# A scale-free attention block and a five-matrix feed-forward on eight cores: the transposed-weight reloads move to SyncE's queue, and one weight copy moves from VectorE to ScalarE

## The chip, the cores and the metric

The kernel runs on the 8 cores of one Trainium2 chip. Every core runs the same program on its own data, without any exchange between cores. The time is the device time of the slowest core in microseconds (us). A core has TensorE (PE: matmuls and, here, also all transposes, which are matmuls against an identity), VectorE (DVE), ScalarE (ACT), GpSimd (POOL) and SyncE (SP, which only issues DMAs here). Each engine runs its own instruction list strictly in the order in which the program wrote it; a DMA is issued by an instruction on POOL, SP or ACT, and lands later, which a semaphore tells.

## What is computed

There are 16384 tokens of 1024 numbers. All cores need the 64x64 matrix `energy` over all tokens; after that, each core owns 2048 tokens.

```
Q, K, V = x wq', x wk', x wv'                    # 64 wide
energy  = K' V                                    # 64 x 64, over all 16384 tokens
x1 = layernorm(x + sqrt(3/64) * Q energy wo')
h  = silu(s1 * (x1 w1')) * (s2 * (x1 w2'))        # 4096 wide
h  = gelu(sh1 * (h h1'))                          # 4096 x 4096 weights
h  = gelu(sh2 * (h h2'))                          # 4096 x 4096 weights
y  = layernorm(x1 + s3 * (h w3'))                 # back to 1024
```

## The kernel before

The tokens of a core are worked in two halves, `h = 0` and `h = 1`, of 1024 tokens each. A half goes through these stages in order:

- `emit_b3(h)`: for 8 tiles of 128 tokens, the attention output, the residual sum and the first layer norm. SyncE loads a tile of x into `X1R` (line 392) and stores the normed tile to `x1s` in device memory (line 422). TensorE transposes the tile into `X1T`.
- `emit_stage1(h)`: 32 output chunks `oc` of 128 hidden units. For each, 16 matmuls for w1 and w2 on tokens 0 to 511 (lines 525 and 533, into `PA`), then 16 on tokens 512 to 1023 (into `PB`). ScalarE applies silu (line 540), VectorE multiplies (line 545) into `HB`.
- `emit_big_stage` three times, for h1 (32 chunks), h2 (32) and w3 (8): 64 matmuls per chunk (line 621), alternating between `PA` and `PB`, and one activation on ScalarE (line 645).
- `make_final_ln`: the last layer norm over 8 tiles.

**First half.** The weights arrive untransposed as f32 and are cast to bf16 by POOL's DMAs into `WSB` (lines 462, 466, 563). TensorE transposes each chunk into the PSUM tiles `PT[0]` and `PT[1]`, and these are copied into one of two slots of `WTB`. In `emit_stage1` the w1 part is copied by VectorE (line 491) and the w2 part by ScalarE (line 495). ScalarE then issues a DMA that stores the transposed chunk to device memory (`wt12`, line 502; `h1t`, `h2t` and `w3t` in the big stages).

**Second half.** Nothing is transposed again. The stored chunk is loaded back into a slot of `WTB`: 512 KB for each of the 32 chunks of `emit_stage1` (line 509) and 1024 KB for each of the 72 chunks of the big stages (line 571). These loads are issued by POOL, whose list holds nothing else then. The load of chunk `oc` waits until the matmuls of chunk `oc - 2` have left the slot, so that it lands while chunk `oc - 1` is computed. TensorE waits for it just before the first matmul of `oc`.

**The last layer norm of the first half** is woven into `emit_stage1(1)` by a hook: before each of the chunks 0, 4, 8, ... 28, `fstep0(oc // 4)` writes one tile of it into the lists. TensorE transposes the tile out of `GB` (line 666), ScalarE copies it to `FT` (line 675), VectorE adds the residual `X1R` (line 693), then `emit_ln` runs: ScalarE (338, 342), VectorE (347, 352), ScalarE's square root (357), VectorE (362, 366, 371). SyncE's list gets, for each tile, first the load of `X1R` (line 683), then a wait for the end of the tile's norm (line 371) and the store of `y` (line 705). The hook is called ahead of everything else that a chunk writes:

```
        for oc in range(HC):
            if hook is not None:
                hook(oc)
            ...
                w('y', 'v', lnv)
            ...
                em('y', lambda s_, th=th, r=r: s_.dma_start(
                    out=y[th * 128:(th + 1) * 128, :],
```

`w(q, src, val)` (line 144) makes engine `q` wait for a semaphore; `'g'` is POOL, `'y'` SyncE, `'t'` TensorE, `'s'` ScalarE and `'v'` VectorE. `light_handoff` puts such waits between stages. In the second half the gate that it gets is the end of all TensorE work of the stage before, so the first load of each big stage starts when the stage before has ended.

Of the kernel before, what the change touches and what calls it, by code (L numbers as in the profile page):

```python
# [16 lines left out]
EC = E // 128  # L17
# [11 lines left out]
def build():  # L29
# [58 lines left out]
    SGP = [EE(nc.semaphore("SGP0")), EE(nc.semaphore("SGP1")),  # L88
           EE(nc.semaphore("SGP2")), EE(nc.semaphore("SGP3"))]
    SYL = [EE(nc.semaphore("SYL0")), EE(nc.semaphore("SYL1"))]  # L90
    SYS = [EE(nc.semaphore("SYS0")), EE(nc.semaphore("SYS1"))]
    SWS = [EE(nc.semaphore("SWS0")), EE(nc.semaphore("SWS1"))]
    SUS = [EE(nc.semaphore("SUS0")), EE(nc.semaphore("SUS1"))]
# [4 lines left out]

    Q = {k: [] for k in "gystv"}
    C = {"l": 0, "g0": 0, "g1": 0, "g2": 0, "g3": 0,  # L100
# [3 lines left out]
    SEM = {"l": SL, "g0": SGP[0], "g1": SGP[1], "g2": SGP[2], "g3": SGP[3],  # L104
           "y0": SYL[0], "y1": SYL[1],
           "z0": SYS[0], "z1": SYS[1],
           "w0": SWS[0], "w1": SWS[1], "u0": SUS[0], "u1": SUS[1],
# [34 lines left out]
    def w(q, src, val):  # L142
        if val > 0:
            em(q, lambda e, s=SEM[src], v=val: e.wait_ge(s, v))

# [4 lines left out]
    def fi(ins, fin, sem=None):  # L150
        if fin:
            ins.then_inc(sem if sem is not None else ST, 1)
        return ins

    QENG = {"l": "g", "g0": "g", "g1": "g", "g2": "g", "g3": "g",
            "y0": "y", "y1": "y",
            "z0": "y", "z1": "y",
            "w0": "s", "w1": "s", "u0": "s", "u1": "s",
# [291 lines left out]
                x1te[tp] = inc('s')  # L450
        return C['s']

    def emit_stage1(h, hook=None):
        wdma = {}; wtp = {}; wte = {}; wte_lo = {}; mmv = {}; sil = {}; hv = {}; cw = {}
        for oc in range(HC):
            if hook is not None:
                hook(oc)
            ro = oc % 2
            if h == 0:
                if oc >= 2:  # L460
                    w('g', 't', wtp[oc - 2])
                em('g', lambda g, oc=oc, ro=ro: g.dma_start(
                    out=WSB[:, ro * 1024:(ro + 1) * 1024],
                    in_=w1[oc * 128:(oc + 1) * 128, :]).then_inc(SGP[ro], 16))
                inc(f'g{ro}', 16)
                em('g', lambda g, oc=oc, ro=ro: g.dma_start(
                    out=WSB[:, 2048 + ro * 1024: 2048 + (ro + 1) * 1024],
                    in_=w2[oc * 128:(oc + 1) * 128, :]).then_inc(SGP[ro], 16))
                wdma[oc] = inc(f'g{ro}', 16)
                w('t', f'g{ro}', wdma[oc])  # L470
                if oc >= 1:
                    w('t', 's', wte[oc - 1])
                    w('t', 'v', wte_lo[oc - 1])
                for c in range(EC):
                    em('t', lambda t, ro=ro, c=c: t.transpose(
                        PT[0][:, c * 128:(c + 1) * 128],
                        WSB[:, ro * 1024 + c * 128: ro * 1024 + (c + 1) * 128], IDB[:]))
                for c in range(EC):
                    em('t', lambda t, ro=ro, c=c: fi(t.transpose(
                        PT[1][:, c * 128:(c + 1) * 128],  # L480
                        WSB[:, 2048 + ro * 1024 + c * 128: 2048 + ro * 1024 + (c + 1) * 128],
                        IDB[:]), c == EC - 1))
                wtp[oc] = inc('t')
                w('v', 't', wtp[oc])
                w('s', 't', wtp[oc])
                if oc >= 2:
                    w('v', 't', mmv[(oc - 2, 1)])
                    w('v', f'w{ro}', cw[oc - 2])
                    w('s', 't', mmv[(oc - 2, 1)])
                    w('s', f'w{ro}', cw[oc - 2])  # L490
                em('v', lambda v, ro=ro: v.tensor_copy(  # L491
                    WTB[:, ro * 2048: ro * 2048 + 1024],
                    PT[0][:, 0:1024]).then_inc(SV, 1))
                wte1 = inc('v')
                em('s', lambda s, ro=ro: s.copy(
                    WTB[:, ro * 2048 + 1024: ro * 2048 + 2048],
                    PT[1][:, 0:1024]).then_inc(SS, 1))
                wte[oc] = inc('s')
                wte_lo[oc] = wte1
                w('s', 'v', wte1)  # L500
                w('s', 's', wte[oc])
                em('s', lambda s, oc=oc, ro=ro: s.dma_start(
                    out=wt12[oc],
                    in_=WTB[:, ro * 2048:(ro + 1) * 2048]).then_inc(SWS[ro], 16))
                cw[oc] = inc(f'w{ro}', 16)
            else:
                if oc >= 2:
                    w('g', 't', mmv[(oc - 2, 1)])
                em('g', lambda g, oc=oc, ro=ro: g.dma_start(
                    out=WTB[:, ro * 2048:(ro + 1) * 2048],  # L510
                    in_=wt12[oc]).then_inc(SGP[ro], 16))
                wdma[oc] = inc(f'g{ro}', 16)
            for g_i in range(2):
                s_ = oc * 2 + g_i
                rp = s_ % 2
                if g_i == 0:
                    if h == 0:
                        w('t', 'v', wte_lo[oc])
                    else:
                        w('t', f'g{ro}', wdma[oc])  # L520
                if s_ >= 2:
                    w('t', 's', sil[s_ - 2])
                    w('t', 'v', hv[s_ - 2])
                for c in range(EC):
                    em('t', lambda t, ro=ro, rp=rp, c=c, g_i=g_i: t.matmul(  # L525
                        PP[rp][:, 0:512],
                        WTB[:, ro * 2048 + c * 128: ro * 2048 + (c + 1) * 128],
                        X1T[:, c * 1024 + g_i * 512: c * 1024 + g_i * 512 + 512],
                        start=(c == 0), stop=(c == EC - 1)))
                if g_i == 0 and h == 0:  # L530
                    w('t', 's', wte[oc])
                for c in range(EC):
                    em('t', lambda t, ro=ro, rp=rp, c=c, g_i=g_i: fi(t.matmul(  # L533
                        PP[rp][:, 512:1024],
                        WTB[:, ro * 2048 + 1024 + c * 128: ro * 2048 + 1024 + (c + 1) * 128],
                        X1T[:, c * 1024 + g_i * 512: c * 1024 + g_i * 512 + 512],
                        start=(c == 0), stop=(c == EC - 1)), c == EC - 1))
                mmv[(oc, g_i)] = inc('t')
                w('s', 't', mmv[(oc, g_i)])
                em('s', lambda s, rp=rp, g_i=g_i, oc=oc: s.activation(  # L540
                    TS1[:, g_i * 512:(g_i + 1) * 512], PP[rp][:, 0:512], AF.Silu,
                    bias=0.0, scale=SC1[:, oc:oc + 1]).then_inc(SS, 1))
                sil[s_] = inc('s')
                w('v', 's', sil[s_])
                em('v', lambda v, rp=rp, g_i=g_i, oc=oc: v.scalar_tensor_tensor(
                    HB[:, oc * 1024 + g_i * 512: oc * 1024 + g_i * 512 + 512],
                    PP[rp][:, 512:1024], SC2[:, oc:oc + 1],
                    TS1[:, g_i * 512:(g_i + 1) * 512],
                    ALU.mult, ALU.mult).then_inc(SV, 1))
                hv[s_] = inc('v')  # L550
        return wtp.get(HC - 1, C['t'])

    def emit_big_stage(wsrc, scl, src_buf, dst_buf, nout, func, cache, h):
        wdma = {}; wtp = {}; wte = {}; mmv = {}; gel = {}; cw = {}; rdv = {}
        for oc in range(nout):
            so = oc % 2
# [10 lines left out]
                    wdma[(oc, half)] = inc(f'g{s_slot}', 16)  # L567
            else:
                if oc >= 2:
                    w('g', 't', mmv[(oc - 2, 3)])  # L570
                em('g', lambda g, oc=oc, so=so, cache=cache: g.dma_start(
                    out=WTB[:, so * H:(so + 1) * H],
                    in_=cache[oc]).then_inc(SGP[so], 16))
                rdv[oc] = inc(f'g{so}', 16)

            def emit_tp(b):
                half = b // 2
# [29 lines left out]
            def emit_mm(b):  # L607
                rp = oc % 2
                if h == 0:
                    w('t', 'v', wte[(oc, b)])  # L610
                elif b == 0:
                    w('t', f'g{so}', rdv[oc])
                if b == 0 and oc >= 2:
                    w('t', 's', gel[oc - 2])
                for j in range(8):
# [117 lines left out]
    for h in range(2):  # L733
# [3 lines left out]
        if h == 0:  # L737
            g1_ = emit_stage1(0)
        else:
            fstep0 = make_final_ln(0)  # L740
            g1_ = emit_stage1(1, hook=lambda oc: fstep0(oc // 4) if oc % 4 == 0 else None)
        light_handoff(g1_)
        g2_ = emit_big_stage(h1, SCH1, HB, GB, HC, AF.Gelu, h1t, h)
        light_handoff(g2_)
        g3_ = emit_big_stage(h2, SCH2, GB, HB, HC, AF.Gelu, h2t, h)
        light_handoff(g3_)
        g4_ = emit_big_stage(w3, SC3, HB, GB, EC, AF.Copy, w3t, h)
        if h == 0:
            light_handoff(g4_)
        else:  # L750
# [42 lines left out]
```

## Time and profile before

| | us |
|---|---|
| median of three runs | 3510.24 |
| the three runs | 3510.24, 3539.15, 3329.22 |
| the profiled execution | 3328.28 |
| its span on the slowest core (core 6) | 3326.7 |
| spans of the eight cores | 3311.9 to 3326.7 |

The profile is one execution, recorded on the slowest core. Its page has the busy time of each engine, the span in 40 slices, the chain of waits that ended last, and groups of instructions by line. The trace behind it also answers for a stretch of time: which instruction ran when, and what ended the idle time ahead of it. Times in it are counted from the start of the span. By these, the stages lie at about 287 to 372 us (`emit_b3(0)`), 372 to 682 (`emit_stage1(0)`), 682 to 1880 (big stages, first half), 1880 to 1965 (`emit_b3(1)`), 1965 to 2214 (`emit_stage1(1)` with the hook), 2214 to 3234 (big stages, second half), and 3234 to the end (last layer norm of the second half). What comes before 287 us is the pass over all 16384 tokens.

### The profile page before, as it was taken

The page shows a single profiled execution, that of the slowest core. Times are in us where ns is not written, and L with a number is a line of the kernel's source. Part 1 is how long each engine was busy: PE and PEld are TensorE (multiplying, and loading weights), DVE is VectorE, ACT ScalarE, POOL GpSimd, SP SyncE. Part 2 cuts the span into 40 slices and gives each one's busy share as a digit, 9 for nine tenths or more (in the row PEclk, how much of TensorE's full clock was granted, in tenths as well). Part 3 has the DMA queues.
Part 4 walks back from the last instruction along what each step waited for, and adds up shares of the span by engine and source line. Part 5 has one row for each costly group of instructions (what it writes and reads, how often), then busy time and mean ns, then how long its engine had stood idle before and what let it go on. Part 6 is the DMA issues. An engine that isn't in the chain of part 4 may idle for free.

```text
span 3326.7 us, 40570 instructions; the slowest of 8 cores (3311.9 to 3326.7 us)
## 1 busy us (share of the span) xinstructions
PE 2855.8 (86%) x16601; PEld 1447.9 (44%) x16601; DVE 448.5 (13%) x833; ACT 527.0 (16%) x630; POOL 243.3 (7%) x460
## 2 busy tenths in 40 slices
PE   5673588889999999999999649989999999999990
PEld 4662244444444444444444324434444444444440
DVE  1112222211111111111111232210000000000002
ACT  4553222210000000000000123320000000000012
POOL 3220011100000000000000000000000000000000
PEclk9886799999999999999999869999999999999995
DMA  8994455556666656655555423222222122222112
GB/s 110 136 135 102 97 110 106 114 109 127 128 131 136 127 123 131 131 127 127 127 126 127 119 96 104 96 92 76 76 76 76 64 78 78 78 78 78 68 57 95
DMA packets 89170, 347.16 MB, mean 104 GB/s; under 512 B 10904, under 2 KB 10976, under 8 KB 70560
## 3 DMA queue, kind: packets, MB, share of 16 engines
q0 software_dynamic: 64800, 218.73, 34.8%
q10 hardware_dynamic: 14976, 92.28, 6.8%
q1 hardware_dynamic: 9216, 33.56, 2.9%
q8 instruction: 138, 2.26, 0.3%
q14 instruction: 40, 0.33, 0.0%
HBM read 361.83 MB, written 109.05 MB: 142 GB/s over the span
## 4 chain that ended last, share of the span: by engine, by line
PE 75%; DVE 5%; DMA 4%; issue 3%; ACT 3%; DVEq 0%; SPq 0%; ACTq 0%; POOL 0%; POOLq 0%
PE PA L621 30%; PE PB L621 29%; PE PT L585 3%; PE PA L525 3%; PE PA L533 3%; PE PB L533 3%; PE PB L525 3%; DMA X1R<-x 2%; DVE WTB L596 1%; DMA X1R<-x1s 1%; ACT TS L540 1%; DVE WTB L491 1%; ACT TS L342 1%; DVE X1F L411 1%; DVE X1F L371 1%
## 5 line engine op out<-in xcount | busy, mean ns | idle before, releaser
L621 PE MATMUL PA<-HB,WTB 128*128 128x512 bf16 x2560 | 571.6, 383 | 12.1 <-DMA WTB<-h1t 6.3
L621 PE MATMUL PB<-HB,WTB 128*128 128x512 bf16 x2560 | 562.3, 379 | 0.0
L621 PE MATMUL PA<-GB,WTB 128*128 128x512 bf16 x2048 | 452.3, 380 | 5.8 <-DMA WTB<-h2t 5.8
L621 PE MATMUL PB<-GB,WTB 128*128 128x512 bf16 x2048 | 449.9, 379 | 0.0
L621 PEld LDWEIGHTS PA<-HB,WTB 128*128 128x128 bf16 x2560 | 250.9, 99 | 312.3 <-issue 25.3
L621 PEld LDWEIGHTS PB<-HB,WTB 128*128 128x128 bf16 x2560 | 248.9, 98 | 292.5
L596 DVE COPY WTB<-PT 128x1024 bf16<-128x1024 bf16 x288 | 192.5, 689 | 990.8 <-PE PT L585 990.7
L621 PEld LDWEIGHTS PA<-GB,WTB 128*128 128x128 bf16 x2048 | 199.7, 98 | 241.9 <-issue 9.6
L621 PEld LDWEIGHTS PB<-GB,WTB 128*128 128x128 bf16 x2048 | 198.9, 98 | 234.2
L585 PE MATMUL PT<-IDB,WSB 128*128 128x128 bf16 x2304 | 164.9, 220 | 53.7 <-DVE WTB L596 44.4
L525 PE MATMUL PA<-X1T,WTB 128*128 128x512 bf16 x512 | 125.8, 390 | 72.0 <-DVE WTB L491 52.7
L585 PEld LDWEIGHTS PT<-IDB,WSB 128*128 128x128 bf16 x2304 | 142.6, 98 | 98.9 <-issue 65.6
L257 PE MATMUL PT<-IDB,XB 128*128 128x128 bf16 x1024 | 91.3, 241 | 78.5 <-DMA XB<-x 68.7
L693 DVE SCALAR_TENSOR_TENSOR X1F<-X1R,FT 128x1024 f32<-128x1024 f32 x12 | 14.7, 1225 | 1045.4 <-DMA X1R<-x1s 1038.1
L265 ACT COPY XT<-PT 128x1024 bf16<-128x1024 bf16 x128 | 129.5, 1012 | 126.2 <-PE PT L257 125.2
L563 POOL DMA_DIRECT2D WSB<-h x128 | 68.9, 538 | 990.4 <-PE PT L585 938.7
L440 PE MATMUL PT<-IDB,X1B 128*128 128x128 bf16 x128 | 16.2, 305 | 135.3 <-DVE X1B L429 135.3
L533 PE MATMUL PA<-X1T,WTB 128*128 128x512 bf16 x512 | 123.4, 385 | 0.0
L525 PE MATMUL PB<-X1T,WTB 128*128 128x512 bf16 x512 | 121.0, 379 | 0.0
L533 PE MATMUL PB<-X1T,WTB 128*128 128x512 bf16 x512 | 120.9, 379 | 0.0
L645 ACT ACTIVATE HB<-PA,SCH 128x1024 bf16<-128x1024 f32 x32 | 35.7, 1114 | 458.5 <-PE PA L621 458.5
L257 PEld LDWEIGHTS PT<-IDB,XB 128*128 128x128 bf16 x1024 | 69.1, 107 | 88.1 <-issue 84.5
(116 smaller groups left out, 1341.9 us busy)
## 6 DMA issues: line engine op xcount, KB each, us to landing
WSB<-h POOLq DMA_DIRECT2D x128, 512.0 KB, 6.3
XB<-x POOLq DMA_DIRECT2D x128, 256.0 KB, 6.1
h1t<-WTB ACTq DMA_DIRECT2D x32, 1024.0 KB, 8.3
h2t<-WTB ACTq DMA_DIRECT2D x32, 1024.0 KB, 8.4
WTB<-h1t POOLq DMA_DIRECT2D x32, 1024.0 KB, 5.1
WTB<-h2t POOLq DMA_DIRECT2D x32, 1024.0 KB, 5.1
WSB<-w POOLq DMA_DIRECT2D x64, 256.0 KB, 6.0
wt<-WTB ACTq DMA_DIRECT2D x32, 512.0 KB, 6.6
```

Of the source, the lines that this page charges most:

```text
L257: em('t', lambda t, r2=r2, r4=r4, c=c: fi(t.transpose(PT[r2][:, c * 128:(c + 1) * 128], XB[:, r4 * E + c * 128: r4 * E + (c + 1) * 128], I ...
L265: em('s', lambda s, r2=r2, r4=r4: s.copy(XT[:, r4 * E:(r4 + 1) * E], PT[r2][:, 0:1024]).then_inc(SS, 1))
L342: em('s', lambda s, r=r, slot=slot, dump=dump: s.activation(dump[:, 0:1024], X1F[:, r * E:(r + 1) * E], AF.Square, bias=0.0, scale=1.0, ac ...
L371: em('v', lambda v, r=r, slot=slot: v.tensor_scalar(X1F[:, r * E:(r + 1) * E], X1F[:, r * E:(r + 1) * E], RS[:, slot:slot + 1], NMR[:, slo ...
L411: em('v', lambda v, r=r: v.scalar_tensor_tensor(X1F[:, r * E:(r + 1) * E], PP[r][:, 0:1024], 1.0, X1R[:, r * E:(r + 1) * E], ALU.mult, ALU ...
L525: em('t', lambda t, ro=ro, rp=rp, c=c, g_i=g_i: t.matmul(PP[rp][:, 0:512], WTB[:, ro * 2048 + c * 128: ro * 2048 + (c + 1) * 128], X1T[:, ...
L533: em('t', lambda t, ro=ro, rp=rp, c=c, g_i=g_i: fi(t.matmul(PP[rp][:, 512:1024], WTB[:, ro * 2048 + 1024 + c * 128: ro * 2048 + 1024 + (c ...
L563: g.dma_start(out=WSB[:, s_slot * 2048:(s_slot + 1) * 2048], in_=wsrc[oc * 128:(oc + 1) * 128, half * 2048:(half + 1) * 2048]).then_inc(SG ...
L585: em('t', lambda t, s_slot=s_slot, b=b, j=j: fi(t.transpose(PT[b % 2][:, j * 128:(j + 1) * 128], WSB[:, s_slot * 2048 + (b % 2) * 1024 + j ...
L596: em('v', lambda v, so=so, b=b: v.tensor_copy(WTB[:, so * H + b * 1024: so * H + (b + 1) * 1024], PT[b % 2][:, 0:1024]).then_inc(SV, 1))
L621: first=first, last=last, src_buf=src_buf: fi(t.matmul(PP[rp][:, g_i * 512:(g_i + 1) * 512], WTB[:, so * H + b * 1024 + j * 128: so * H + ...
L645: s.activation(dst_buf[:, oc * 1024:(oc + 1) * 1024], PP[rp][:, 0:1024], func, bias=0.0, scale=scl[:, oc:oc + 1]).then_inc(SS, 1))
```

## The change

Two things change, and one follows from them.

- In `emit_stage1(0)`, the copy of the w1 part out of `PT[0]` is done by ScalarE, just ahead of its copy of the w2 part. TensorE and the DMA that stores the chunk wait for ScalarE alone.
- In the second half, all reloads of transposed weights (lines 509 and 571) are issued by SyncE, with semaphores of their own (`SR`). They are written into SyncE's list at the same place in the program as they were into POOL's, thus in `emit_stage1(1)` behind what the hook writes.
- The waits that `light_handoff` gave to POOL are written for SyncE ahead of the first two loads of a stage (`ygate`, `ent_w`). For `emit_stage1(1)` the gate is the same as before, the end of the first half's matmuls.

```diff
@@ emit_stage1 @@
-    def emit_stage1(h, hook=None):
+    def emit_stage1(h, hook=None, ygate=0):
+        ent_w = {0: C['w0'], 1: C['w1']}
...
                 if oc >= 1:
                     w('t', 's', wte[oc - 1])
-                    w('t', 'v', wte_lo[oc - 1])
...
                 wtp[oc] = inc('t')
-                w('v', 't', wtp[oc])
                 w('s', 't', wtp[oc])
                 if oc >= 2:
-                    w('v', 't', mmv[(oc - 2, 1)])
-                    w('v', f'w{ro}', cw[oc - 2])
                     w('s', 't', mmv[(oc - 2, 1)])
                     w('s', f'w{ro}', cw[oc - 2])
-                em('v', lambda v, ro=ro: v.tensor_copy(
+                em('s', lambda s, ro=ro: s.copy(
                     WTB[:, ro * 2048: ro * 2048 + 1024],
-                    PT[0][:, 0:1024]).then_inc(SV, 1))
-                wte1 = inc('v')
+                    PT[0][:, 0:1024]).then_inc(SS, 1))
+                wte1 = inc('s')
...
                 wte_lo[oc] = wte1
-                w('s', 'v', wte1)
                 w('s', 's', wte[oc])
...
             else:
                 if oc >= 2:
-                    w('g', 't', mmv[(oc - 2, 1)])
-                em('g', lambda g, oc=oc, ro=ro: g.dma_start(
+                    w('y', 't', mmv[(oc - 2, 1)])
+                else:
+                    w('y', 't', ygate)
+                    w('y', f'w{ro}', ent_w[ro])
+                em('y', lambda s_, oc=oc, ro=ro: s_.dma_start(
                     out=WTB[:, ro * 2048:(ro + 1) * 2048],
-                    in_=wt12[oc]).then_inc(SGP[ro], 16))
-                wdma[oc] = inc(f'g{ro}', 16)
+                    in_=wt12[oc]).then_inc(SR[ro], 16))
+                wdma[oc] = inc(f'r{ro}', 16)
...
                     if h == 0:
-                        w('t', 'v', wte_lo[oc])
+                        w('t', 's', wte_lo[oc])
                     else:
-                        w('t', f'g{ro}', wdma[oc])
+                        w('t', f'r{ro}', wdma[oc])
@@ emit_big_stage @@
                 if oc >= 2:
-                    w('g', 't', mmv[(oc - 2, 3)])
-                em('g', lambda g, oc=oc, so=so, cache=cache: g.dma_start(
+                    w('y', 't', mmv[(oc - 2, 3)])
+                else:
+                    w('y', 't', ygate)
+                    w('y', f'w{so}', ent_w[so])
+                em('y', lambda s_, oc=oc, so=so, cache=cache: s_.dma_start(
                     out=WTB[:, so * H:(so + 1) * H],
-                    in_=cache[oc]).then_inc(SGP[so], 16))
-                rdv[oc] = inc(f'g{so}', 16)
+                    in_=cache[oc]).then_inc(SR[so], 16))
+                rdv[oc] = inc(f'r{so}', 16)
@@ the stages @@
-            g1_ = emit_stage1(1, hook=lambda oc: fstep0(oc // 4) if oc % 4 == 0 else None)
+            g1_ = emit_stage1(1, hook=lambda oc: fstep0(oc // 4) if oc % 4 == 0 else None,
+                              ygate=pre_b3_gate)
```

## Rows read from the trace of the kernel before

**Rows 1.** The page: busy time of engines, and TensorE's granted clock in 40 slices.
```profile
PE 2855.8 (86%) x16601; PEld 1447.9 (44%) x16601; DVE 448.5 (13%) x833; ACT 527.0 (16%) x630; POOL 243.3 (7%) x460
PEclk9886799999999999999999869999999999999995
```

**Rows 2.** Stretches A:B: length, each engine's busy time, granted clock, DMA share.
```profile
1965.00:1994.80 29.80, 29.79 (x137) 13.66 (x138) 8.05 (x14) 8.73 (x13) 1.61 (x3) 0.94 0.28 93
1994.80:2027.20 32.40, 29.89 (x137) 13.32 (x136) 8.72 (x15) 10.48 (x15) 2.22 (x4) 0.95 0.31 98
2182.80:2213.60 30.80, 27.97 (x132) 12.39 (x129) 8.71 (x15) 10.54 (x16) 1.81 (x3) 1.00 0.21 69
1888.00:1965.00 77.00, 13.86 (x76) 6.96 (x77) 25.96 (x58) 18.70 (x36) 0.00 (x0) 0.50 0.33 108
1965.00:2214.00 249.00, 230.70 (x1088) 104.62 (x1088) 69.04 (x119) 82.77 (x119) 16.74 (x31) 0.98 0.29 96
```

**Rows 3.** In order of time, one chunk of the first half's stage 1: start, length.
```profile
511.48 0.61 PE L479 MATMUL PT<-IDB,WSB 128*128 128x128 bf16 x8
512.08 0.75 DVE L545 SCALAR_TENSOR_TENSOR HB<-PB,SC,TS 128x512 bf16<-128x512 f32 x1 [2.70 <-ACT TS L540]
512.29 1.01 ACT L495 COPY WTB<-PT 128x1024 bf16<-128x1024 bf16 x1 [0.31 <-PE PT L479]
512.75 0.68 DVE L491 COPY WTB<-PT 128x1024 bf16<-128x1024 bf16 x1
513.79 1.89 PE L525 MATMUL PA<-X1T,WTB 128*128 128x512 bf16 x8 [1.71 <-DVE WTB L491]
515.52 1.89 PE L533 MATMUL PA<-X1T,WTB 128*128 128x512 bf16 x8
```

**Rows 4.** DMA issues: size, and median us from issue to landing.
```profile
WTB<-h1t POOLq DMA_DIRECT2D x32, 1024.0 KB, 5.1
h2t<-WTB ACTq DMA_DIRECT2D x32, 1024.0 KB, 8.4
WTB<-wt POOLq DMA_DIRECT2D x32, 512.0 KB, 3.7
X1R<-x SPq DMA_DIRECT2D x16, 512.0 KB, 4.2
X1R<-x1s SPq DMA_DIRECT2D x16, 512.0 KB, 4.4
```

**Rows 5.** In order of time, layer-norm step 1 inside the second half's stage 1.
```profile
1994.78 0.61 PE L666 MATMUL PT<-IDB,GB 128*128 128x128 bf16 x8
1995.23 1.89 PE L525 MATMUL PA<-X1T,WTB 128*128 128x512 bf16 x8
2002.50 0.81 DVE L371 TENSOR_SCALAR X1F<-X1F,RS,NMR 128x1024 f32<-128x1024 f32 x1
2003.45 0.34 SPq L705 DMA_DIRECT2D y<-X1F  x1
2003.88 0.38 SPq L683 DMA_DIRECT2D X1R<-x1s  x1
2004.81 2.38 PE L525 MATMUL PA<-X1T,WTB 128*128 128x512 bf16 x8 [2.51 <-DVE HB L545]
```

**Rows 6.** In order of time, the start of the second half's stage 1.
```profile
1965.82 3.22 PE L525 MATMUL PA<-X1T,WTB 128*128 128x512 bf16 x8
1972.66 0.34 SPq L705 DMA_DIRECT2D y<-X1F  x1
1974.76 0.54 POOL L509 DMA_DIRECT2D WTB<-wt  x1 [92.96 <-PE PB L533]
```

**Rows 7.** The chain of waits in order of time: TensorE after a wait, and steady.
```profile
1966.02 3.02 PE PA L525 x8
...
2004.81 2.38 PE PA L525 x8
2007.19 2.92 PE PA L533 x8
2010.11 1.73 PE PB L525 x8
...
2213.93 5.47 DMA WTB<-h1t
2219.54 16.41 PE PA L621 x64
2235.96 13.81 PE PB L621 x64
```

More of the change, by code:

```diff
@@ L90, in build @@
     SYL = [EE(nc.semaphore("SYL0")), EE(nc.semaphore("SYL1"))]
+    SR = [EE(nc.semaphore("SR0")), EE(nc.semaphore("SR1"))]
     SYS = [EE(nc.semaphore("SYS0")), EE(nc.semaphore("SYS1"))]
@@ L104, in build @@
     SEM = {"l": SL, "g0": SGP[0], "g1": SGP[1], "g2": SGP[2], "g3": SGP[3],
+           "r0": SR[0], "r1": SR[1],
            "y0": SYL[0], "y1": SYL[1],
@@ L155, in build @@
     QENG = {"l": "g", "g0": "g", "g1": "g", "g2": "g", "g3": "g",
+            "r0": "y", "r1": "y",
             "y0": "y", "y1": "y",
@@ L551, in emit_stage1, with emit_big_stage @@
         return wtp.get(HC - 1, C['t'])
-    def emit_big_stage(wsrc, scl, src_buf, dst_buf, nout, func, cache, h):
+    def emit_big_stage(wsrc, scl, src_buf, dst_buf, nout, func, cache, h, ygate=0):
+        ent_w = {0: C['w0'], 1: C['w1']}
         wdma = {}; wtp = {}; wte = {}; mmv = {}; gel = {}; cw = {}; rdv = {}
@@ L611, in emit_mm @@
                 elif b == 0:
-                    w('t', f'g{so}', rdv[oc])
+                    w('t', f'r{so}', rdv[oc])
                 if b == 0 and oc >= 2:
@@ L740, in build @@
             fstep0 = make_final_ln(0)
-            g1_ = emit_stage1(1, hook=lambda oc: fstep0(oc // 4) if oc % 4 == 0 else None)
+            g1_ = emit_stage1(1, hook=lambda oc: fstep0(oc // 4) if oc % 4 == 0 else None,
+                              ygate=pre_b3_gate)
         light_handoff(g1_)
-        g2_ = emit_big_stage(h1, SCH1, HB, GB, HC, AF.Gelu, h1t, h)
+        g2_ = emit_big_stage(h1, SCH1, HB, GB, HC, AF.Gelu, h1t, h, ygate=g1_)
         light_handoff(g2_)
-        g3_ = emit_big_stage(h2, SCH2, GB, HB, HC, AF.Gelu, h2t, h)
+        g3_ = emit_big_stage(h2, SCH2, GB, HB, HC, AF.Gelu, h2t, h, ygate=g2_)
         light_handoff(g3_)
-        g4_ = emit_big_stage(w3, SC3, HB, GB, EC, AF.Copy, w3t, h)
+        g4_ = emit_big_stage(w3, SC3, HB, GB, EC, AF.Copy, w3t, h, ygate=g3_)
         if h == 0:
```

1 row of the table C is left out of this document.

## The prediction

> **What bounds the kernel now.** I read the page's busy times first, to see which engine could set the end. TensorE is busy 86% of the span, VectorE 13%, ScalarE 16%, POOL 7% [rows 1]. So TensorE sets the time, and what matters is when it stands still and at which clock it runs. The granted clock is near full almost everywhere and lower at the layer norms between the halves [rows 1]. Next I read the stretches of the stage that the change touches most, the second half's stage 1 with its woven layer norm: it takes 249.0 us with TensorE busy for 230.7 [rows 2]. Then I read the timelines of one chunk and of one layer-norm step, to see which wait ends last [rows 3, 5]. The DMA list says how long each reload takes to land, and the chain of waits shows what TensorE pays when it starts again after standing still [rows 4, 7].
>
> A steady group of 8 matmuls takes 1.73 us [rows 7], so a stage 1 chunk (four groups) takes 6.91 us, and a big-stage chunk 13.81 us [rows 7]. A reload is issued about two chunks ahead of its use, so it has nearly one whole chunk in which to land: 3.7 us against 6.91, and 5.1 against 13.81 [rows 4]. The reloads cost nothing today, except at the three starts of the big stages, where TensorE waits the whole landing (5.47 us at the first, [rows 7]).
>
> **Part 1: the w1 copy goes to ScalarE (first half, 32 chunks).** Taken alone, ScalarE's copy is slower: 1.01 us against VectorE's 0.68 [rows 3]. But VectorE's list has the product of the chunk before in front of it (512.08, 0.75 us), so its copy starts at 512.75 and ends at 513.43, while ScalarE starts its copy at 512.29 and ends at 513.30 [rows 3]. In the new order ScalarE's first copy is the w1 copy. Its start is set by silu and the transposes, as now, so I leave it at 512.29. TensorE starts 0.36 us after the end of the copy now (513.79 after 513.43). With the same step after 513.30 it starts at 513.66: 0.13 us earlier. The second copy ends a little over a microsecond later, near 514.3, and is needed only after 8 matmuls (1.73 us), at 515.4: it is covered. If that cover were gone, it would cost the overlap's 1.0 us a chunk; the cover is 1.1 us. ScalarE's store of the chunk is issued 1 us later, with two chunks of time before its slot is reused. The sum is 32 times -0.13, so **-4 us**. The bounds: if VectorE's queue were not in the way, the swap would cost 0.33 us a chunk, +11; if TensorE started as soon after the copy as it does after other releases (0.14, from 2219.54 less the landing at 2213.93 + 5.47), it would bring 0.35 a chunk, -11. I take the value that the timeline gives.
>
> **Part 2: the reloads of stage 1, second half, move into SyncE's list.** All 32 loads of line 509 move, each with its wait. SyncE's list there holds 8 loads of `X1R`, and 8 stores of `y`, each behind a wait for line 371. The hook writes these ahead of the load of chunk 4k. So SyncE cannot issue that load before layer-norm step k is finished. But step k begins with transposes that stand on TensorE just before the matmuls of chunk 4k. This is the point of the whole case: the load that used to be issued one chunk earlier is now issued only after TensorE has reached the place where it needs it. Behind the waiting instruction are queued the store of `y`, the loads 4k and 4k+1, and later loads; who waits is TensorE.
>
> The price of a step, counted from the start T of its transposes (1994.78 in step 1, [rows 5]):
>
> - The `y` store is issued at 2003.45, T + 8.67. SyncE's next DMA follows 0.43 later (2003.88), T + 9.10. That next DMA is now the reload. Nothing in this chain waits for the matmuls of chunk 4k, so it takes as long as today.
> - Its landing: 512 KB issued by SyncE took 4.2 and 4.4 us in the median [rows 4]. In both cases it followed a 512 KB store in the same list, as here. I take 4.4, since a second reload is issued right behind it. The row of POOL's own 512 KB reload, 3.7, is the lower bound; the upper is 6.
> - TensorE starts 0.14 after a landing (as above): T + 13.64.
> - It comes back at the lower clock. After the waits in the trace, the first groups were longer than steady ones by 1.3 us (1966.02, 3.02 against 1.73), 1.84 (2.38 + 2.92 less twice 1.73) and 2.60 (16.41 less 13.81) [rows 7]. The granted clock was 0.50 in the stretch before 1965 [rows 2], thus the 1.2 GHz level. I take 2.2 a step, between 1.3 and 2.6.
> - Then four chunks: 27.65.
>
> The block of four chunks thus takes 13.64 + 2.2 + 27.65 = 43.5 us. Today it takes 30.8 in a block at full clock, in which a 2.5 us wait for VectorE's product (line 545) is contained, and 32.4 in step 1, where that wait also lowered the clock [rows 2, 5]. That wait vanishes: ScalarE and VectorE have finished the norm before the matmuls start. So five blocks at 12.7, and steps 1 and 2 at about 11.2 each: 86 us. Step 0: SyncE stores `y` at 1972.66, so the reload goes out at 1973.1 and TensorE starts at 1977.65 in place of 1965.82 [rows 6], 11.8 later, plus 0.9 for the clock: 12.7. Together **+98.6 us**.
>
> The other chunks (4k+1, +2, +3) stay covered: 4k+1 is issued right behind 4k; the rest wait for matmuls only, and have 6.91 us less about 0.7 until the issue for a landing of 4.4. The next `X1R` load is behind the reload of 4k+3, two chunks before it is needed. POOL's list, which the loads leave, had nothing else that would go faster.
>
> A rule of the Trainium skill speaks for the move. The page "DMA: Bandwidth & Descriptors", section "Latency and other measured facts", gives a first byte after about 0.6 us for DMAs issued from SyncE and ScalarE, and about 1 us for those from GpSimd. By it the landing would be 0.4 us shorter than POOL's, 3.3 in place of 4.4, and the eight steps 9 us cheaper. The trace does not agree: the same 512 KB took 3.7 from POOL and 4.2 to 4.4 from SyncE [rows 4].
>
> **Part 3: the reloads of the big stages (72 loads of 1024 KB).** Inside a stage the wait is for matmuls only, and SyncE's list holds nothing else, so the loads are hidden as long as they land within 13 us. No row shows such a load from SyncE. The bounds are 5.1 (POOL's) and 8.4 (ScalarE's stores of this size) [rows 4]: hidden at both. If the cover were gone, each microsecond over it would cost 69 us. At the three stage starts the landing is bare. I take SyncE's 4.3 plus 1.4, the step from 512 to 1024 KB on POOL (5.1 less 3.7): 5.7 against 5.1, less some 0.3 for the shorter issue, so **+1 us** in all, between -3 and +10.
>
> **Sum.** The profiled execution took 3328.28 us, its span 3326.7. 3328.3 - 4 + 98.6 + 1 = 3423.9, so **3424 us**, 1.029 of before. The median of the three runs shown is 3510.24, and the fastest, 3329.22, agrees with the profiled one. My number belongs beside these two; it would be compared with the median only by the ratio.
>
> **Rivals.**
>
> *The reload is not late* (not slower). This holds if SyncE's DMA queue lets the reload go ahead of the `y` store's wait, or if the wait is over by the time TensorE arrives. It decides at a landing before T + 0.5: then nothing of part 2 is left, and the time is 3328 - 4 + 1, about 3325. Against it: SyncE issues everything in list order in the trace, and the store never goes before line 371 ends (2002.50 + 0.81, store at 2003.45, [rows 5]). Chance 0.07.
>
> *The stall is much shorter* (within 2%), since the norm chain runs faster with the matmuls standing still, or since other cores' idle time makes landings quicker. To come under 3395, a step must cost less than 8.7 in place of 12.3. The chain has no wait for TensorE after the transposes, and a landing at the bound of 3.7 takes off only 0.7. Chance 0.05.
>
> *The clock stays low for long after each stall.* If the whole first chunk ran at half speed, a step would cost 6.9 in place of 2.2, +38: 3461. For it: eight stalls of 13 us, each near 40 us from the next. Against: three restarts lost at most 2.6 [rows 7]. Chance 0.06.
>
> *Reloads of 1024 KB from SyncE are not hidden.* At a landing of 15 us, behind 0.7 us until the issue, 69 loads would each be 1.9 us late, +131: 3555. The slowest row of this size is 8.4 [rows 4]. Chance 0.03.
>
> **How the numbers follow.** The first case holds 0.79. Its own range: landings and clock between their bounds move eight steps by -13 to +16, the copies by -7 to +15, the stage starts by -4 to +9; hardly all at once, so 3405 to 3447. The range that holds 8 in 10 need leave out only the rivals at the ends: I take 3400 to 3455. Slower by over 2% (above 3395, about what a measurement of this kernel can tell from no change) is 0.79 + 0.06 + 0.03 = 0.88; within 2% is 0.05 and nearly all of the first rival, 0.11 together; faster by over 2% is 0.01, since no term of the sum could bring 67 us.
>
> **What would show it.** In the profile after: TensorE's wait ahead of line 525 names the DMA from `wt`, eight times, near 12.7 us each; SyncE's list shows `y` store, then two reloads 0.4 apart, then a bare landing of about 4.4; the wait for line 545 is gone; the second half's stage 1 takes some 348 us in place of 249; `emit_stage1(0)` is shorter by 4. Wrong would be: reloads issued ahead of the `y` store, a second-half stage 1 near 249 us, or waits inside the big stages. What I could most easily have mis-sized is the clock after each stall, and the landing.

## The result: 3 % slower, lost at eight places

| | us |
|---|---|
| the changed kernel, median of 8 runs | 3432.8 |
| the kernel before, median of 10 runs | 3329.32 |
| ratio | 1.0308, 95% interval 1.0292 to 1.0324 |
| profiled execution of the changed kernel, its span | 3435.01, 3433.4 |

The ratio compares only runs in which no die ran at a lower granted clock than the other; two of the three runs shown ahead of the prediction (3510.24 and 3539.15) and two of the eight here were slowed so.

The view of waits of the changed kernel (who waited for whom: us in total, times, longest us), in the stretch from 1960 to 2325 us, the second half's stage 1:

```profile
PE PA L528 <- DMA WTB<-wt: 114.0, 8, 15.3
```

The wait for a reload stands there eight times and did not stand there at all before. The wait for VectorE's product (line 545 in the kernel before), 17.6 us in 7 times, is gone. In the stretches (length, busy times, granted clock, DMA share), against [rows 2]:

```profile
2008.80:2053.40 44.60, 29.73 (x138) 13.35 (x136) 8.80 (x15) 10.59 (x15) 0.00 (x0) 0.85 0.21 71
2274.90:2320.00 45.10, 29.92 (x137) 13.25 (x135) 8.80 (x15) 10.59 (x15) 0.00 (x0) 0.85 0.19 59
1965.50:2320.00 354.50, 240.34 (x1088) 107.48 (x1088) 69.69 (x119) 82.88 (x118) 0.00 (x0) 0.84 0.21 71
```

A block of four chunks with its norm step takes 44.6 us in place of 32.4 (step 1), and 45.1 in place of 30.8 (step 7). The stage takes 354.5 us in place of 249.0. The two spans differ by 106.7 us, and this one stage by 105.5 to 106: the rest of the program takes about as long as before. The same holds on every core. Counted from the first transpose of step 0 to the end of the stage's matmuls, the stage takes 351 to 354 us on the eight cores in place of 246 to 248. The same instructions are on TensorE (x1088 in both); it is the time between them that grew.

One step in order of time, on the slowest core (start, length, in brackets the idle time ahead), against [rows 5]:

```profile
2008.86 0.61 PE L673 MATMUL PT<-IDB,GB 128*128 128x128 bf16 x8
...
2016.58 0.81 DVE L375 TENSOR_SCALAR X1F<-X1F,RS,NMR 128x1024 f32<-128x1024 f32 x1
2017.52 0.34 SPq L712 DMA_DIRECT2D y<-X1F  x1
2017.96 22.30 SPq L512 DMA_DIRECT2D WTB<-wt  x4
...
2024.34 3.44 PE L528 MATMUL PA<-X1T,WTB 128*128 128x512 bf16 x8 [14.87 <-DMA WTB<-wt]
```

With T at 2008.86, the store of `y` goes out at T + 8.66 and the reload at T + 9.10, to a hundredth what the rows of before gave. TensorE starts at T + 15.48. Before, it started 0.45 us after T.

### The profile page after: what moved, and what is told of

It is laid out like the page before. It is cut to its first block, busy times and chain, and to the rows that moved or that the text cites. A ratio compares the mean times of both kernels' runs of the same rounds, so it can differ in the third digit from the quotient of the medians.

```text
span 3433.4 us, 40447 instructions; the slowest of 8 cores (3413.3 to 3433.4 us)
## 1 busy us (share of the span) xinstructions
PE 2867.0 (84%) x16601; PEld 1454.5 (42%) x16601; DVE 429.9 (13%) x801; ACT 557.0 (16%) x662; POOL 186.8 (5%) x356
## 4 chain that ended last, share of the span: by engine, by line
PE 75%; DMA 6%; DVE 4%; ACT 3%; issue 2%; SPq 0%; DVEq 0%; ACTq 0%; POOL 0%; POOLq 0%
PE PA L628 29%; PE PB L628 28%; PE PA L528 4%; PE PA L536 3%; PE PT L592 3%; PE PB L536 3%; PE PB L528 3%; DMA X1R<-x 2%; DVE WTB L603 1%; DMA WTB<-wt 1%; ACT WTB L492 1%; DMA X1R<-x1s 1%; DVE X1F L375 1%; ACT TS L346 1%; DVE X1F L700 1%
## 5 line engine op out<-in xcount | busy, mean ns | idle before, releaser
L528 PE MATMUL PA<-X1T,WTB 128*128 128x512 bf16 x512 | 135.5, 412 | 164.6 <-DMA WTB<-wt 114.0
L528 PEld LDWEIGHTS PA<-X1T,WTB 128*128 128x128 bf16 x512 | 50.1, 103 | 230.2 <-issue 185.5
L536 PE MATMUL PA<-X1T,WTB 128*128 128x512 bf16 x512 | 122.8, 383 | 0.0
```

The costliest lines, as they stand in the source:

```text
L528: em('t', lambda t, ro=ro, rp=rp, c=c, g_i=g_i: t.matmul(PP[rp][:, 0:512], WTB[:, ro * 2048 + c * 128: ro * 2048 + (c + 1) * 128], X1T[:, ...
L536: em('t', lambda t, ro=ro, rp=rp, c=c, g_i=g_i: fi(t.matmul(PP[rp][:, 512:1024], WTB[:, ro * 2048 + 1024 + c * 128: ro * 2048 + 1024 + (c ...
```

## Where in the change the loss is

The first three experiments take the change apart.

**Only the reloads of stage 1.** The kernel before, with nothing but this edit (and `SR`, its semaphores, and the gate):

```diff
-                    w('g', 't', mmv[(oc - 2, 1)])
-                em('g', lambda g, oc=oc, ro=ro: g.dma_start(
+                    w('y', 't', mmv[(oc - 2, 1)])
+                else:
+                    w('y', 't', ygate)
+                    w('y', f'w{ro}', ent_w[ro])
+                em('y', lambda s_, oc=oc, ro=ro: s_.dma_start(
...
```

> The kernel before with only the 32 reloads of the second half's stage 1 moved into SyncE's list. My theory: this one edit carries the whole loss, so the ratio is 1.033, a little above the full change (1.031), since the gains of the copy and of the stage starts are missing. Rival: the loss needs the other edits too (the copy, or the big stages' reloads on SyncE), then it stays under 1.025.

Measured 3422.46 us, a single run that can be compared, against 3317 to 3322 for the kernel before. So the ratio is about 1.031, without an interval, and one run can't tell it from the 1.033 that was expected. In the trace TensorE waits 105.7 us for `wt`, 8 times. This edit alone carries the loss.

**Everything but the reloads of stage 1.** The changed kernel with line 512's loads back on POOL, as in the kernel before.

> The changed kernel with only the 32 reloads of the second half's stage 1 back on POOL; the copy on ScalarE and the 72 reloads of the big stages on SyncE stay. My theory: the whole loss comes from the 32 reloads, so this is 3326 us, within 0.3% of the kernel before, and the second half's stage 1 takes 249 us again. Rival: loads issued by SyncE cost time wherever they stand, then the big stages keep a part of the loss and the time stays over 3345.

Measured 0.9973 (0.9955 to 0.9990), 3310.67 us against 3321.66. No loss is left: the 72 reloads of the big stages on SyncE cost nothing. It is 9 us faster than the kernel before. Under 2 of them are the copy's (next experiment), and about 2 lie in the big stages of the second half (1118 us on average over the cores in place of 1120).

The other 5 to 6 stand at the very end of the program, after the last store of `y` has landed, where nothing but the closing of the engines' lists is left. POOL's list has two closing instructions (DRAIN). The first is where the pass over all tokens ends and takes 1534 ns in each kernel; the second ends the program. The rows give the shortest, median and longest in ns and the first and last start in us, for the kernel before, this kernel and the changed kernel:

```profile
L114 POOLq DRAIN  x2: 1534/4384/7234, 285.4 to 3319.3; - x2
L117 POOLq DRAIN  x2: 1354/1444/1534, 278.6 to 3305.7; - x2
L117 POOLq DRAIN  x2: 1534/4710/7887, 286.9 to 3425.3; - x2
```

The one at the end takes 7.23 us before, 1.35 here and 7.89 in the changed kernel, the same on all eight cores. It differs between kernels that issue different DMAs from POOL (8.54 us with the stores of `y` there, 4.62 with only stage 1's reloads moved away). By what rule, no run shows.

TensorE's bare landings at the three stage starts, which were 6.3, 5.8 and 5.8 us before, are here (its waits):

```profile
PE PA L625 <- DMA WTB<-h1t: 6.4, 1, 6.4
PE PA L625 <- DMA WTB<-w3t: 5.5, 1, 5.5
PE PA L625 <- DMA WTB<-h2t: 5.0, 1, 5.0
```

**Only the copy.** The kernel before with `em('v', ... v.tensor_copy(` of the w1 part made `em('s', ... s.copy(`, and its waits.

> The kernel before with only the w1 copy of the first half's stage 1 moved from VectorE to ScalarE. My theory: the copy on ScalarE ends 0.14 us earlier in each of 31 chunks, because VectorE's list had a product in front of it, so the time is 4 us below the kernel before, about 3325. Rival: ScalarE's slower copy (1.01 us against 0.68) lies bare, +0.33 us in 32 chunks, 11 us above the kernel before.

> The copy alone once more, since the first comparison left 0.9991 with an interval that holds 1. My theory stays: 4 us below the kernel before (0.9988), with a chunk of the first half's stage 1 at 9.53 us in place of 9.66. Rival: +11 us (1.003).

The ratios were 0.9991 (0.9977 to 1.0005) and 1.0015 (0.9981 to 1.0048). The timing can't tell this edit from no change, and the first of them rules out the rival's 1.003. The trace of the second is sharper. From the first transposes of the stage to those of the last chunk it took 303.5 us before (372.7 to 676.2), and 299.5 with the copy alone (365.9 to 665.4), 4.0 less; the changed kernel has 299.3. A chunk in the kernel with the copy alone, in order of time (compare [rows 3]):

```profile
503.56 0.75 DVE L540 SCALAR_TENSOR_TENSOR HB<-PB,SC,TS 128x512 bf16<-128x512 f32 x1 [2.70 <-ACT TS L535]
503.77 1.01 ACT L487 COPY WTB<-PT 128x1024 bf16<-128x1024 bf16 x1 [0.31 <-PE PT L478]
504.68 1.02 ACT L491 COPY WTB<-PT 128x1024 bf16<-128x1024 bf16 x1
505.14 1.89 PE L520 MATMUL PA<-X1T,WTB 128*128 128x512 bf16 x8 [1.57 <-ACT WTB L487]
506.86 1.89 PE L528 MATMUL PA<-X1T,WTB 128*128 128x512 bf16 x8
```

TensorE's wait ahead of the first group is 1.57 us in place of 1.71, by an engine whose copy is 0.33 slower: VectorE's product (503.56) no longer stands in front of it. The second copy ends at 505.70 and is needed at 506.86.

But more than half of the gain is lost again right behind the stage. POOL's first load of h1's weights waits for the landing of the stage's last transposed chunk, and ScalarE issues that store behind its second copy, 0.73 us later than before, counted from the last transpose. The chain of waits there, in the kernel before and in the kernel with the copy alone:

```profile
678.36 2.95 DMA wt<-WTB
```
```profile
668.33 4.52 DMA wt<-WTB
...
673.38 0.53 POOL WSB L558
673.91 7.33 DMA WSB<-h
```

The store also takes longer to land: 4.6 us on average over the cores, in place of 2.95. From the last matmul of the stage to the first one of h1 it takes 7.9 us on average in place of 5.4. It is 8.0 to 8.2 in the changed kernel and in six further kernels with the copy on ScalarE, and 5.5 in the one above that keeps it on VectorE. So the copy brings 4 us in its stage and gives back 2.5 behind it. What is left is under 2 us, which agrees with the timings.

## Is it SyncE, or the place in SyncE's list?

The three kernels here have every reload on SyncE and the change's other edits; they differ in where the wait for the norm stands.

**The store behind both reloads.** The norm step keeps its load of `X1R` where it is, and its wait and store come after chunk 4k+1's reload:

```diff
-            if hook is not None:
-                hook(oc)
+            if hook is not None and oc % 4 == 0:
+                late_store = hook(oc)
...
                 wdma[oc] = inc(f'r{ro}', 16)
+                if oc % 4 == 1:
+                    late_store()
```

> The changed kernel with all reloads on SyncE, but in SyncE's list the wait for the norm and the store of y are written behind the reloads of chunks 4k and 4k+1. My theory: the loss is the place in the list and nothing else, so TensorE's waits for the reload vanish and the time is 3326 us. Rival: SyncE's own issue and landing are the cause, then reloads are still late and the time stays above 3380.

Measured 0.9991 (0.9981 to 1.0002). The loss is gone with all 104 reloads still on SyncE.

**The store in another list.** The wait and the store of `y` go into POOL's list (`em('g', ...)`, with semaphores of their own); SyncE's list keeps the rest.

> The changed kernel with only the wait for the norm and the store of y, in the norm steps inside stage 1, moved from SyncE's list to POOL's, which is empty there. My theory: it is the wait ahead of the reload that costs, so the time falls to that of the kernel with the store behind two reloads, ratio 0.999. Rival: the loads of X1R in the same list hold the reloads back, then a loss of over 1% stays.

Measured 0.9989 (0.9978 to 1.0001). So the loads of `X1R`, which are still among the reloads, do no harm; the wait and the store do. The two are parted further below.

**The store between the two reloads.** As the first, with `if oc % 4 == 0: late_store()` behind the reload: 4k is in time, 4k+1 is not.

> The changed kernel with the wait for the norm and the store of y written behind the reload of chunk 4k, but still ahead of that of 4k+1. My theory, delay by place in the list: reload 4k is in time, 4k+1 goes out at T + 9.1, lands in 5.6 and TensorE starts chunk 4k+1 at T + 15.0, where the kernel before starts it at T + 10.0; with 1.9 us for the clock in the blocks that ran at full clock before, 6 us a step, 8 steps: 48 us above the kernel before, ratio 1.014. Rival, that what counts is only whether the store is ahead of any reload: the full loss, ratio 1.03; or that one chunk of lead is enough: ratio 1.00.

Measured 1.0138 (1.0122 to 1.0155), 3364.31 us, where 1.014 was worked out. TensorE waits 49.0 us for `wt`, 8 times. The list of SyncE and the chain of waits, around step 2 (T at 2032.53):

```profile
2041.20 0.34 SPq L715 DMA_DIRECT2D y<-X1F  x1
2041.63 14.98 SPq L512 DMA_DIRECT2D WTB<-wt  x3
```
```profile
2041.63 4.89 DMA WTB<-wt
...
2046.88 3.57 PE PA L530 x8
2050.45 2.31 PE PA L538 x8
```

The reload behind the store goes out at T + 9.10 again, and TensorE starts chunk 4k+1 at T + 14.35, where it started at T + 10.03. It then loses 2.4 us more at the lower clock (3.57 + 2.31 less 3.46). That 1.014 was met to the digit is in part luck: T + 15.0 and 1.9 us were put in, an earlier start and a dearer clock came out. The three places, ratios 0.999, 1.014 and 1.031, follow the same arithmetic with one term changed: when the blocked reload is needed.

## The two sizes: the clock and the landing

**The clock.** The changed kernel with matmuls that nobody reads, in the time in which TensorE would stand still:

```diff
             if hook is not None:
                 hook(oc)
+                if oc % 4 == 0:
+                    for k in range(64 if oc else 48):
+                        em('t', lambda t: t.matmul(
+                            PM[:, 0:512], IDB[:], X1T[:, 0:512],
+                            start=True, stop=True))
```

> The changed kernel with 48 (step 0) or 64 (steps 1 to 7) matmuls of 128x512 into an unused PSUM tile, between the transposes of a norm step and the wait for the reload; their results are not used. They take 13.8 us at full clock in a wait of 14.3 to 15.9. My theory: TensorE comes back at 2.4 GHz, so the first two groups of matmuls lose nothing where they lose 1.87 us on average now; with the last steps a little delayed, the time is 13 us below the changed kernel, ratio 1.027. Rival: the restart costs nothing that can be bought back, or the filler delays the norm, ratio 1.031 or more.

Measured 1.0269 (1.0251 to 1.0288), 13 us below the changed kernel. The chain of waits, first in the changed kernel and then in this one, around the restart:

```profile
2106.49 6.42 DMA WTB<-wt
2112.90 0.35 issue
2113.25 3.36 PE PA L528 x8
2116.61 1.73 PE PA L536 x8
```
```profile
2042.44 13.81 PE PM L465 x64
2056.26 1.75 PE PA L533 x8
2058.00 1.73 PE PA L541 x8
```

The group after a stall takes 3.36 us in place of 1.73, that after the filler 1.75. In the eight restarts on the slowest core of the changed kernel the loss is 1.6 to 2.2 us, 1.89 on average. On the other seven cores it is larger, 2.0 to 2.9 us on the average of a core. One restart on core 0:

```profile
2000.53 4.73 DMA WTB<-wt
2005.26 0.35 issue
2005.61 3.57 PE PA L528 x8
2009.18 2.70 PE PA L536 x8
```

With the filler no core loses anything there. The granted clock says the same: 0.76 from 2024.3 to 2031 in the changed kernel, so that the 1.2 GHz level holds for a part of it, and 1.00, the 2.4 GHz level, from 2056 to 2063 with the filler. About 13 us of the loss are thus the clock by the ratios. The stage itself is some 17 us shorter (334 to 337 us on the eight cores in place of 351 to 354). The rest is the standing still itself.

**The landing.** The wait for the norm stays where the change has it; only the store itself is issued behind both reloads (`w('y', 'v', lnv)` ahead, `late_store()` after).

> The changed kernel with the wait for the norm left where it is, ahead of the reloads of 4k and 4k+1, but the store of y itself behind both. The landing that lies bare was 5.6 us on average where I took 4.4. Theory A: the store ahead in the same queue makes the difference, then the landing is about 4.6, and with the issue 0.4 us earlier the time is 8 times 1.4, 11 us below the changed kernel, ratio 1.027. Theory B: the second reload behind it shares the DMA engines, then the landing stays near 5.6 and the time falls by 3 us at most, ratio 1.030.

Measured 1.0268 (1.0250 to 1.0286), 13 us below the changed kernel. SyncE's list of this kernel at step 2:

```profile
2050.59 0.79 SPq L512 DMA_DIRECT2D WTB<-wt  x2
2051.53 0.34 SPq L715 DMA_DIRECT2D y<-X1F  x1
```

The bare landings on the slowest core average 4.05 us here and 5.62 in the changed kernel. On cores 0 to 6 they are 3.6 (3.5 to 3.8) against 4.7 (4.5 to 4.9). So about 1.1 us of a landing comes from the 512 KB store that was issued 0.43 us ahead of it in the same list, and the second reload behind it adds little: theory A. Whether the list matters or only the traffic at the same time, this doesn't settle. In the kernel before, the seven reloads that POOL issued 0.6 us ahead of SyncE's store of `y` and 1 us ahead of its load of `X1R` took 4.8 us on the slowest core, the others 3.7, though no list was shared. Eight times 1.1, and eight times the 0.43 by which the reload is issued sooner, are 12 of the 13 us. By the Trainium skill, "DMA: Bandwidth & Descriptors", section "Latency and other measured facts", SyncE's loads should start sooner than POOL's. The trace shows no gain for whole reloads: 3.6 without a store ahead, POOL's median before was 3.7 [rows 4], and with a store ahead 4.7.

## A version that is faster than both

At the start of each big stage of the second half TensorE waits 5 to 6 us for the first reload, since its gate is the end of the stage before [rows 7]. `WTB` has two slots; one is free a chunk earlier. The next kernel has the store of `y` behind two reloads, lets the chunks of the big stages begin in the slot that comes free first, and gates each first reload on that slot alone:

```diff
-            so = oc % 2
+            so = (oc + (1 if pre is not None else 0)) % 2
...
-                    w('y', 't', ygate)
+                    w('y', 't', pre[oc] if pre is not None else ygate)
...
+        last['mm'] = (mmv[(nout - 2, 3)], mmv[(nout - 1, 3)])
```

> As the one before, and the first reload of each big stage of the second half goes into the slot that comes free first, so that it is issued before the stage ahead of it ends. My theory: at three stage starts a wait of 6.3 us shrinks to about 2 (the last activation), and the restart at the lower clock (about 2.6 us) mostly goes, so 3 times 7, about 21 us below the one before: 3305, faster than both kernels. Rival: the last activation and the handoff leave most of the wait, then it gains under 8 us.

Measured 0.9938 (0.9923 to 0.9953), 3300.47 us, 18 us below the kernel with the store behind two reloads, where 21 were worked out.

The same with stage 1's reloads on POOL:

> The copy on ScalarE, the reloads of stage 1 on POOL as before the change, those of the big stages on SyncE, and the early first reload of each big stage. My theory: the 9 us that the kernel with stage 1's reloads back on POOL brought (ratio 0.9973) and the 21 less 3 that the early first reload brought are independent, so 27 us below the kernel before: ratio 0.992. Rival: both save the same wait, then it is no better than 0.994.

Measured **0.9906 (0.9890 to 0.9921), 3288.91 us**, 31 us below the kernel before, where 27 were worked out. The start of the first big stage in its chain of waits, against 2213.93 to 2235.96 in [rows 7]:

```profile
2201.18 1.74 PE PB L535 x8
...
2203.79 0.76 DVE HB L547
2204.55 0.24 issue
2204.79 13.97 PE PA L628 x64
```

TensorE stands still for 1.9 us, until silu and the product of the last chunk are done, and comes back at full clock: the first chunk takes 13.97 us in place of 16.41.

With stage 1's reloads on POOL the kernel is better than with them on SyncE by 6 us (0.9973 against 0.9991) and by 11 us (0.9906 against 0.9938). Two places make it up. The first is the end of the program: POOL's closing instruction takes 1.35 us in both kernels with these reloads on POOL and 7.89 in both with them on SyncE, 6.5 us. The second is the start of stage 1, 2 to 3 us on average over the cores. SyncE's list still has the layer norm between the halves ahead of the first reload; POOL's has nothing there and loads it far ahead. In the kernel with the store behind two reloads this first landing is left bare, in its chain of waits:

```profile
1957.48 4.87 DMA WTB<-wt
1962.49 3.57 PE PA L530 x8
1966.06 3.00 PE PA L538 x8
```

## What the prediction had right, and which steps failed

The mechanism of the loss held, and so did the ratio: 1.029 was forecast, 1.031 measured. Three steps of the sum failed: the base on which the time was put, the price of a step in part 2 (on the slowest core its landing), and what follows the stage in part 1, which was put at nothing.

**The base.** The sum starts from the profiled execution, 3328.3 us, and gives 3424, while the median shown for the kernel before was 3510.24. The prediction says that its number belongs beside 3328.28 and 3329.22, but gives no time for the median that was shown; there, 1.029 makes 3612. Held against 3510.24 as it stands, 3424 is a gain of 2.5%, where the change lost 3.1%. The further runs showed which base was the right one: the kernel before has a median of 3329.32, and the changed kernel 3432.8.

**Part 1, the copy: -4 forecast, -4.2 in its stage** (303.5 to 299.3), by the mechanism named: VectorE's product was in front of the copy. The step that failed is the store of the chunk. The prediction saw that it is issued 1 us later and put this at nothing, since its slot is reused two chunks on. At the end of the stage the first weights of h1 wait for it, and that costs 2.5 us again. So the part brings under 2 us and not 4.

**Part 2, the reloads of stage 1: +98.6 forecast, +106 measured** on the slowest core. By terms, in us, averaged over a core's steps (the issue and the third row hold for steps 1 to 7):

| | forecast | slowest core | the other seven |
|---|---|---|---|
| issue of the reload | T + 9.10 | T + 9.10 | T + 9.10 |
| landing | 4.4 | 5.62 | 4.5 to 4.9 |
| from landing to TensorE | 0.14 | 0.35 | 0.35 to 0.46 |
| loss at the lower clock | 2.2 | 1.89 | 2.0 to 2.9 |

On the slowest core the mis-sized term is the landing: 8 times 1.2 is 9.8 us. The forecast took the median of SyncE's 512 KB loads behind a store. On the other seven cores that was nearly right (4.7), but it did not make their stage shorter: cores 0 and 1, with landings of 4.7 and 4.6 us, took 354.4 and 353.7 us for it, where the slowest core took 354.4. There the clock cost more instead. From T until TensorE is back in step after the restart, counted by the starts of its groups in steps 1 to 7, all eight cores need 16.5 to 16.8 us, where the forecast had 15.84. So the whole restart was priced 0.7 to 1.0 us too low on every core, and how this divides between landing and clock differs from core to core. Why the slowest core had the longer landing is open: in the kernel with only stage 1's reloads moved, the same core 7 landed in 4.5 and was not the slowest. The step from the landing to TensorE is 0.2 longer than after the single wait of a big stage. A likely reason, which no run tests, is that more waits stand here ahead of the matmuls in TensorE's list, as they do after the copy (0.36); the prediction used that row for the copy and not for this. The clock's term was 0.3 too high on this core. The three together are 9.8 + 1.5 - 2.5 = 8.8; 7.5 were missing.

**Part 3, the big stages: +1 forecast, 0 measured.** The landing of 1024 KB from SyncE is 0.5 us longer at a stage start (6.08, 5.51 and 5.52 against 5.47, 5.04 and 5.01), and the issue comes 0.5 sooner after the last matmul (0.12 against 0.64). Inside the stages no wait appeared; the median landing was 4.8 us where a chunk has 13. Not in the sum at all was the closing of POOL's list, 0.7 us longer.

**The rivals.** That the reload would not be late fell with the timeline: SyncE issued it 0.43 to 0.48 us after the store in every step. A much shorter stall fell with the same rows, since the norm took as long with TensorE idle as with it busy (8.66 against 8.67 us). The clock cost 1.6 to 2.2 us a restart on the slowest core and at most 3.1 on the others, not the 6.9 of a whole chunk at half speed. Loads of 1024 KB stayed hidden.

## What to carry to other kernels

Before a DMA is moved to another engine's list, write out what stands ahead of it there, and for each wait ask whether it is released by work that comes after the point where the moved DMA is needed. Here the wait was released by a chain that began at that very point, so a prefetch of one chunk turned into a full landing plus the chain, 14 us a time. The cure was the order, not the engine: two reloads ahead of the waiting store, and the whole loss was gone.

## What the runs showed of the hardware

- A 512 KB load from SyncE landed 1.1 us later (4.7 against 3.6 us) when a 512 KB store had been issued 0.4 us ahead of it from the same list. A load from POOL with a store and a load from SyncE right behind it took 4.8 us against 3.7.
- ScalarE's slower copy (1.01 us against 0.68) gave an earlier start of TensorE, 1.57 us of wait in place of 1.71, since the faster engine's list was occupied. Of 4 us gained so in the stage, 2.5 were lost behind it, where a store that ScalarE now issued 0.7 us later held up the next load.
- Idle waits of 14 us cost TensorE 1.9 us each at the lower clock when it came back on one core, and 2.0 to 2.9 on the seven others. Matmuls without use in that time bought 13 us back over eight waits.
- The closing instruction of POOL at the end of the program took 1.35 to 8.54 us, the same on all eight cores of a kernel, and changed with the DMAs that POOL had issued.
